# Self and cross attention as one stream of 120 steps, with the join and the query products between them as side work

## The reference

```python
h1 = _ln(x, n1_g, n1_b)
x = _attn(h1, h1, q1, k1, v1, o1_w, o1_b, heads) + x        # self: 512 keys
h2 = _ln(x, n2_g, n2_b)
x = _attn(h2, context, q2, k2, v2, o2_w, o2_b, heads) + x   # cross: 1024 keys
h3 = _ln(x, n3_g, n3_b)
...
ff = a * jax.nn.gelu(g, approximate=False) @ ff_w2 + ff_b2
return ff + x
```

## Time and profile before

| | us |
|---|---|
| median of 3 runs | 935.91 (933.89 to 936.53) |
| the profiled execution | 930.57 (span 928.8) |
| TensorE busy, share of the span | 844.5, 91% |
| VectorE busy | 617.0, 66% |
| ScalarE busy | 470.6, 51% |
| self steps (first exponential to the last values) | 375.5 to 489.8 |
| join and query products | 492.4 to 531.9 |
| cross prologue | 534.9 to 564.2 |
| cross steps | 564.2 to 783.3 |

### The profile page before, as it was taken

The page is one execution under the profiler, slowest core; times in us unless marked ns, Lnnn a source line. Parts: engine busy times, 40 slices in busy tenths (PEclk is TensorE's granted clock), DMA queues, the critical chain, the costliest instruction groups (busy, mean ns, idle before and its releaser), DMA issues.

```text
span 928.8 us, 11352 instructions
## 1 busy us (share of the span) xinstructions
PE 844.5 (91%) x4148; PEld 462.4 (50%) x4148; DVE 617.0 (66%) x1158; ACT 470.6 (51%) x682; POOL 78.2 (8%) x107
## 2 busy tenths in 40 slices
PE   4769989999999999999988699999999998699998
PEld 3646744444466675333324443333333333378988
DVE  4245547777583646799956597999999971656132
ACT  4523445454543441567785304766677777555030
POOL 3200000400004021000000300000000000120000
PEclk9979989999998997799999756999999999889999
DMA  6938768542401074222134320222222001400000
GB/s 222 271 102 239 230 169 254 174 116 60 118 26 41 21 231 124 65 70 70 37 66 73 109 72 1 53 53 53 53 53 53 2 2 43 198 1 1 29 1 29
DMA packets 30967, 83.18 MB, mean 90 GB/s; under 512 B 5173, under 2 KB 9213, under 8 KB 28607
## 3 DMA queue, kind: packets, MB, share of 16 engines
q1 hardware_dynamic: 30110, 79.71, 30.3%
q0 software_dynamic: 800, 2.73, 1.1%
HBM read 56.12 MB, written 25.89 MB: 88 GB/s over the span
## 4 chain that ended last, share of the span: by engine, by line
PE 60%; DVE 25%; DMA 6%; ACT 4%; issue 3%; POOL 1%; SPq 0%; DVEq 0%; ACTq 0%; POOLq 0%
PE PS L859 17%; PE PS L802 13%; DVE maxp L961 10%; PE PS L1376 8%; PE PS L553 8%; PE PS L839 6%; DVE negm L961 5%; PE PS L1388 4%; DMA k_d<-split 2%; PE PS L1200 2%; DMA ca_nat<-in_ca 2%; DVE turned L994 1%; ACT probs L925 1%; DVE out_t L1005 1%; DMA q_sl<-msplit 1%
## 5 line engine op out<-in xcount | busy, mean ns | idle before, releaser
L925 ACT ACTIVATE probs<-PS 128x1024 f32<-128x1024 f32 (+1 forms) x336 | 311.7, 971 | 150.0 <-PE PS L839 144.6
L961 DVE TENSOR_REDUCE maxp<-PS 128x1 f32<-128x512 f32 x448 | 280.1, 679 | 47.0 <-PE PS L802 46.0
L802 PE MATMUL PS<-k_sl,q_sl 48*128 48x512 f32 (+3 forms) x640 | 262.1, 489 | 24.4 <-DMA q_sl<-q_d 11.8
L802 PEld LDWEIGHTS PS<-k_sl,q_sl 48*128 48x128 f32 (+2 forms) x640 | 119.2, 199 | 201.5 <-DVE maxp L961 121.5
L839 PE MATMUL PS<-q_sl,k_sl 50*128 50x512 f32 (+3 forms) x672 | 203.2, 433 | 8.2 <-ACT probs L925 5.2
L961 DVE TENSOR_REDUCE negm<-PS 128x1 f32<-128x512 f32 (+1 forms) x192 | 121.0, 679 | 27.7 <-PE PS L802 27.6
L839 PEld LDWEIGHTS PS<-q_sl,k_sl 50*128 50x128 f32 (+2 forms) x672 | 102.6, 191 | 55.8 <-ACT probs L925 24.4
L859 PE MATMUL PS<-probs,v2c 128*32 128x512 f32 x640 | 87.4, 615 | 1.0
L591 DVE TENSOR_TENSOR split<-PS,split 128x512 fp32r<-128x512 f32 (+3 forms) x54 | 34.6, 649 | 47.9 <-ACT split L568 47.9
L859 PE MATMUL PS<-probs,v0c 128*64 128x512 f32 (+1 forms) x256 | 62.6, 610 | 0.0
L568 ACT CAST split<-PS 128x512 fp32r<-128x512 f32 (+3 forms) x54 | 29.8, 553 | 60.2 <-PE PS L553 51.7
(11 more groups left out here) (178 smaller groups left out, 981.0 us busy)
## 6 DMA issues: line engine op xcount, KB each, us to landing
k_d<-split SPq DMA_DIRECT2D x20, 512.0 KB, 3.6
q_d<-split SPq DMA_DIRECT2D x12, 512.0 KB, 3.1
k_sl<-k_d SPq DMA_DIRECT2D x8, 640.0 KB
k_sl<-k_d SPq DMA_DIRECT2D x40, 128.0 KB
q_sl<-q_d SPq DMA_DIRECT2D x40, 128.0 KB
k_sl<-k_d SPq DMA_DIRECT2D x20, 256.0 KB
w_raw<-in_ff_w SPq DMA_DIRECT2D x1, 3840.0 KB, 11.6
k_d<-split SPq DMA_DIRECT2D x10, 256.0 KB, 3.9
```

The lines of the kernel that those rows point to most:

```text
L802: nc.tensor.matmul(PS[0:a.qt, SBANKS[k % 3], 0:cn], q_view(g)[f:f + a.rows, j // a.stack, q * a.qt:(q + 1) * a.qt], k_view(g)[f:f + a.rows ...
L925: nc.scalar.activation(probs[0:a.size[t], x % PRING, :, 0:a.nq], PS[0:a.size[t], 2 * (x % 2):2 * (x % 2) + 2, 0:a.nq], ACT.Exp, scale=a.sc ...
L961: nc.vector.tensor_reduce((maxp if nch > 1 else negm)[0:a.qt, g.turn, o:o + 1], PS[0:a.qt, SBANKS[k % 3], 0:a.chunks[c][1]], AX.X, ALU.max ...
```

## The change

`S_SELF` and `S_CROSS` become one stream `S_REST` of 40 + 80 steps. The lead goes from 8 to 12 at step 39: four chunks (47 to 50) are issued there in a row, a "burst", after the values of step 39 and before the scores of step 40; chunks 40 to 46, also of cross attention, lie in steps 32 to 38. The first join's work and the query products are side tasks behind the maxima of named steps, in the maxima's three banks (`S1` = 20, `X0` = 40):

TensorE, the new order of a step:

```diff
             for s in range(len(st.steps)):
+                burst = st.burst_at(s)
+                if burst:
+                    for p in range(2):
+                        values(*st.steps[s], p)
+                for c in burst:
+                    maxima([c])
+                    flips([c])
+                    beside(st.burst_side.get(c, []))
...
                 maxima(st.chunks_at(s), 3)
                 flips(st.chunks_at(s))
+                beside(st.side.get(s, []))
```

A bank used by a side task is free when VectorE has added the product, when ScalarE has copied the turn, or when VectorE has subtracted a query's high part:

```diff
-                pe.wait_ge(st.score_free if by == "item" else st.flipped, n)
...
+                if by == "product":
+                    pe.wait_ge(join1.added, join1.base + n)
+                if by == "turn":
+                    pe.wait_ge(join1.ready, join1.base + n)
+                if by == "query":
+                    pe.wait_ge(crossp.low, n)
```

More of the change, by code:

```diff
@@ L863, in values, with beside @@
             mm.then_inc(st.used, 1)
+        def beside(tasks):
+            for kind, n in tasks:
+                k = st.side_use[kind, n]
+                bank = SBANKS[k % 3]
+                if kind == "product":
+                    pe_side_product(pe, n, bank, lambda: bank_free(k))
+                if kind == "turn":
+                    pe_side_turn(pe, n, bank, lambda: bank_free(k))
+                if kind == "query":
+                    pe_side_query(pe, n, bank, lambda: bank_free(k))
         for x in range(st.lead):
@@ L895, in pe_attention @@
                 maxima(st.chunks_at(s), 2, 3)
-                for p in range(2):
-                    values(*st.steps[s], p)
+                if not burst:
+                    for p in range(2):
+                        values(*st.steps[s], p)
                 maxima(st.chunks_at(s), 3)
                 flips(st.chunks_at(s))
+                beside(st.side.get(s, []))
     def act_attention(act, st, side=None):
@@ L963, in reduce, with maxima @@
                                     AX.X, ALU.max, negate=nch == 1).then_inc(st.score_free, 1)
-        def maxima(chunks, normalising=None):
-            if normalising is not None and normalising[1] == 0:
-                normalise(*normalising)
-                normalising = None
+        def maxima(chunks, first=(), second=(), third=()):
+            for part in first:
+                part()
+            todo = {1: list(second), 2: list(third)}
             for c in chunks:
@@ L1180, in build, with pe_side_product @@
     join2 = Join(3, w_out2, 2, 2, False)
+    side_stat, side_aggr = sem("side_stat"), sem("side_aggr")
+    side_root, side_inv = sem("side_root"), sem("side_inv")
+    def pe_side_product(pe, t, bank, bank_free):
+        b, c = t // 4, (t % 4) * 128
+        if t == 0:
+            pe.wait_ge(loaded_o1, 16)
+        if t % 4 == 0:
+            pe.wait_ge(A_SELF.out_done, join1.groups * (b + 1))
+        bank_free()
+        for g in range(join1.groups):
+            mm = nc.tensor.matmul(PS[:, bank, 0:D], out_t[:, b * join1.groups + g, c:c + 128], w_out1[:, g, :],
+                                  start=(g == 0), stop=(g == join1.groups - 1))
+        mm.then_inc(join1.product, 1)
```

287 lines of the change are left out of this document (206 added, 81 removed).

## The result

The changed kernel took 940.0 us (median of 17 runs, 935.5 to 944.3), the kernel before 936.3 (17 runs beside it): ratio 1.0043, 95% interval 1.0024 to 1.0061. A gain of 16 us was forecast and a loss of 4 measured, above the range of 906 to 934. The profiled execution of after has a span of 938.7 us and a time of 940.54.

The account below looks back on a forecast made before the run. Plain steps of 2.70 us were taken as balanced, TensorE working 2.45, VectorE 2.4; VectorE bound the prologue. 64.4 - 24.3 - 1 - 22.1 - 1 = 16.0 us gained: 914.6 profiled, 920.0 at the median, range 906 to 934.

Parts of the forecast that it names:

- the clock, a term of 1 us: Around the burst: a stretch at the low clock level costs 1 us, nothing at the least, 4 at most.
- The walk through the steps: Side work followed step by step through engines and bank waits: 24.3 us in batch 0, 22.1 in batch 1.
- Part 1: Self step 32 to cross step 43: merged stages take 44.0 us in place of 108.4, gaining 64.4 before side work.
- Part 3, batch 0: Self steps 21 to 29: products, turns and query products as side work cost 24.3 us.
- The store wait: Step 29: query 2's copy waits for query 0's store, queued behind group 8's loads, costing 3.3 us beyond the product.
- Part 4: Burst and cross steps to 49: batch 1's side work and the last self group's transposes cost 22.1 us.
- Rival (c): Clock stays low through steps 21 to 48, costing 24 us: 8 slower, 944 at the median; chance 0.08.
- Rival (b): Every wait between engines 0.5 us longer over some 25 side tasks, or group 10's load late: 12 us more, 932; chance 0.17.
- The rule weighed: ScalarE table switches cost 1.28 us plus a 1.38 drain each: up to 5.5 us more, about 925.5; a row spoke against it.
- Rival (d): Each ScalarE table switch drains, two of four or all on the path: 923 to 925.5; chance 0.04.
- Rival (a): Side work overlaps better, banks free sooner, costing only 29.3 us: gain 35, 900.6 at the median; chance 0.18.
- Rival (e): Cross maxima don't start before the join, and the burst grows to a prologue: about 20 us stay, 940; chance 0.05.

Follow-up runs that it names:

- kernel with the store first: The changed kernel with SyncE issuing the stores of queries 0 and 1 ahead of the loads of group 8's maxima: 0.9994 of the kernel before.
- the best version: The changed kernel with query stores first, side tasks spread, products and queries mid-step, statistics behind each add, two extra matmuls per burst maximum: 929.8 us, 0.9915 of before.

## Why the prediction was wrong, step by step

The miss is 20.0 us at the medians. By kernels that leave work out it is 3.9 in the merged stages (57.2 for 61.1) and 16.1 in the side work (61.2 for 45.1). By the table of stages it is 5.5 (a wrong row) + 6.9 (batch 0) + 1.9 (burst) + 7.8 (cross steps) - 0.3. The two sums differ by 1.8, less than what the unchanged stages of two profiled executions differ by: from the end of step 56 on and ahead of step 21, after took 5.1 us more than before, of which about 1.0 is the weight split. The profiled execution of before, at 930.57, is faster than all of its 17 later runs (931.25 to 942.59), so differences are taken from the medians and stages, not from that time.

Two steps of the prediction failed: a row read as the wrong step, 5.5 us, and above all the clock, a term of 1 us that measures about 14.5 (an estimate, worked out below). The walk through the steps was right to 1 or 2 us wherever the clock was up.

- **Part 1, the stages that fall together: right in sum, wrong in its left end.** Steps 32 to 39 took 20.3 (forecast 20.6) and the merged kernel gained 57.2. The failing step is "Between self step 32 (465.62) ... and cross step 43 (574.01) ... lie 108.4 us": the row is that of step 30. Counting steps from a row whose number is sure, and once more from the other side, would have shown it.
- **Part 3, batch 0: 24.3 forecast, 31.2 measured, and most of the excess is the clock.** Steps 21 to 29, counted by TensorE's first scores, took 56.1 and not 50.7: steps 21 to 23, at the high level, 17.7 for a forecast of 18.6, but 24 to 27 took 26.1 for 19.6. The forecast had the clock at 1.00 there; it fell. Three executions have the same work in self steps 21 to 32 (but for the root's table, missing in the second) and differ in the clock, the first number behind the busy times: after, the kernel without that table, and that with the extra matmuls (which lie behind this stretch).

```profile
442.10:506.10 64.00, 54.16 (x242) 24.18 (x242) 40.79 (x83) 32.91 (x48) 5.92 (x7) 0.87 0.23 61
```

```profile
442.70:509.50 66.80, 56.92 (x242) 26.11 (x242) 40.79 (x83) 30.49 (x46) 6.18 (x7) 0.82 0.21 58
```

```profile
445.00:513.60 68.60, 60.12 (x242) 27.20 (x242) 40.80 (x83) 32.88 (x47) 5.91 (x7) 0.78 0.20 54
```

  Low time is 17.1, 23.9 and 30.7 us, so each us of it costs about 0.35. Taken back to none, after's 64.0 become some 58 against the 57.1 forecast: about 6 of the 6.9 us are the clock, an estimate from single executions. What is left, about 1, is all that the walk's hand-overs can have been short of. Steps 24 to 26, with two turns a step, are where they may be: they took 17.9 in after for a forecast of 13.0, with 10.0 of low time. The store wait was foreseen; its price of 3.3 can't be checked to better than the 4.6 above.
- **Part 4, burst and batch 1: 1.9 and 7.8 over, nearly all of it the clock.** The walk (nine plain steps at 25.5, and +11.2) gave 36.7 for steps 41 to 49; they took 41.9. The burst took 25.3 for 23.4. With the two extra matmuls in the burst, the same cross steps 40 to 56 ran with no low time. The windows of after, and of that kernel:

```profile
551.70:619.20 67.50, 60.64 (x295) 25.10 (x294) 48.31 (x90) 41.73 (x57) 11.45 (x13) 0.86 0.18 41
```

```profile
557.00:618.10 61.10, 53.60 (x295) 22.32 (x294) 48.19 (x90) 41.71 (x56) 11.44 (x13) 1.00 0.20 45
```

  The same work took 61.1 and not 67.5, for 18.3 us of low time less: 0.35 us for each again. Burst and cross steps together took 84.2 there, against 82.1 forecast without the term for the clock, and 92.8 in after.
- **The clock, the term of 1 us.** This is the worst sized of the terms. In the burst a single product takes 3.25 us, where a pair takes 3.50 in step 21 at the high level, and VectorE waits 3.27 for the next maximum:

```profile
536.41 3.25 PE L1284 MATMUL PS<-w_out,out_t 128*128 128x320 f32 x6 [0.23 <-DVE maxp L1024]
...
540.13 0.69 DVE L1024 TENSOR_REDUCE maxp<-PS 128x1 f32<-128x512 f32 x1 [3.27 <-PE PS L842]
```

  The low level then stays through steps 40 to 42 (0.52 from 552 to 567). The kernel with the store first has the same code there, and its clock is 0.95 behind the burst. Exponentials of steps 40 and 41, in after and then in that kernel:

```profile
551.67 1.94 ACT L986 ACTIVATE probs<-PS 128x1024 f32<-128x1024 f32 x2 [15.19 <-PE PS L879]
558.29 1.94 ACT L986 ACTIVATE probs<-PS 128x1024 f32<-128x1024 f32 x2 [4.68 <-PE PS L879]
```

```profile
553.44 1.94 ACT L986 ACTIVATE probs<-PS 128x1024 f32<-128x1024 f32 x2 [15.19 <-PE PS L879]
557.96 1.94 ACT L986 ACTIVATE probs<-PS 128x1024 f32<-128x1024 f32 x2 [2.58 <-PE PS L879]
```

  6.62 against 4.52; over steps 40 to 46 it is 31.3 against 26.7. In sum: about 6 in batch 0, 2.2 in the burst (25.3 for 23.1 with the extra matmuls, which had 9.0 us of low time less there) and 6.4 behind it, 14.5 where 1 was forecast and 4 allowed. After has 51 us of low time between steps 21 and 56, in pieces. Before had 48, of them 39 ahead of step 40 in its prologue, where VectorE was the bound and the low level cost nothing that shows. The low time was not made, it was moved to where TensorE is the bound. The medians agree in kind: over after's 17 runs, which spread over 9 us, the span grows by about 0.3 us for each us of low time.
- **Rival (c)** had this mechanism, at 0.08. It wanted the low level through steps 21 to 48; that it came in pieces makes its 24 us some 14.5, and the row of part 1 gives the rest of the loss. **Rival (b)**, every hand-over longer than in the walk, at 0.17 and 12 us, is not what happened: about 1 us is left for it in batch 0 and up to 2 in batch 1.
- **The rule weighed.** The Trainium skill (ScalarE: Activation LUTs, What ACT_TABLE_LOAD costs) adds a drain of 1.38 us to each load. No row here shows it (the root begins 0.01 us behind its load), and leaving all four loads out changed neither step clock. Rival (d) falls.
- **Rival (a)**, better overlap, falls: the side work cost 61 and not 29. **Rival (e)** falls: the cross maxima do start in step 32, and the burst has 16 of them.
- **The range.** The gain of 16 was the difference of two large terms. The first, 64.4, was 5.5 too high, 9% of it; the second, 45.1 for the side work of both batches, came out at 61.2, 36% more. The 14 us above the forecast allowed for 31% on the second alone, and for nothing on the first.

What stays open: why the clock falls in batch 0. From 471.0 to 484.6 it was low in after, and nearly every kernel with turns in batch 0 has a low stretch about there; the one with products alone has none. So no execution of this code has steps 24 to 26 at the high level throughout, and their split into clock and hand-overs rests on the price of 0.35. And whether the extra matmuls help at all at the medians: the best version lies 2.3 us under the same kernel without them, and the intervals overlap.

## What to carry to other kernels

Work put into a pipeline whose engines hand over through three banks in strict order does not hide in their idle time, since each task passes through the engines one after the other: a walk that adds up the hand-overs gave 45 us, where the same work as a block took 39.5 (45.1 with its gaps), and at the high level of the clock the walk held to 1 or 2 us. The runs paid 61, because TensorE was at the low level for part of the side work. So price such a move in two parts: the hand-overs, and then the clock, with about 0.3 to 0.35 us for each us of low time in steps that TensorE bounds. A stretch in which TensorE only feeds VectorE drops to the low level for free (0.51 in the old prologue); output products placed in it take nearly twice as long (3.25 us for one, 3.50 for two at the high level), so they belong where the clock is up. Test the two halves apart (the stages merged with no side work, then the side work added kind by kind), since the gain is a small difference of two large numbers, and compare stage times only together with the low time of each execution.

## What the runs showed of the hardware

- **The low level costs this stream about 0.35 us per us**: batch 0 took 64.0, 66.8 and 68.6 us at a granted clock of 0.87, 0.82 and 0.78, the cross steps 61.1 and 67.5 at 1.00 and 0.86, with the same work. **A plain self step at the low level takes 4.2 us, not 2.7**, where rival (c) had taken 3.56. ScalarE in the kernel with the store first, start of the self stage:

```profile
388.86 1.94 ACT L986 ACTIVATE probs<-PS 128x1024 f32<-128x1024 f32 x2 [2.32 <-PE PS L879]
393.02 1.94 ACT L986 ACTIVATE probs<-PS 128x1024 f32<-128x1024 f32 x2 [2.22 <-PE PS L879]
397.18 1.94 ACT L986 ACTIVATE probs<-PS 128x1024 f32<-128x1024 f32 x2 [2.22 <-PE PS L879]
```

- **A VectorE instruction took three times as long beside a GpSimd one that shares no data with it.** The normalised rows take 0.44 us, but once 1.40, ending 0.19 behind a GpSimd subtraction of the query input's low part; the change moved that subtraction to GpSimd. Nine more of these kernels show such a row, of 1.23 to 1.40 us, always beside that subtraction; the kernel before shows none. In after:

```profile
472.43 0.44 DVE L1353 TENSOR_SCALAR xhat<-resid,mv,rstd 128x320 f32<-128x320 f32 x1
...
473.01 1.40 DVE L1353 TENSOR_SCALAR xhat<-resid,mv,rstd 128x320 f32<-128x320 f32 x1
```

```profile
472.93 1.29 POOL L1400 TENSOR_TENSOR act_low<-act_t,x_high 128x512 fp32r<-128x512 f32 x1 [0.47 <-ACT x_mixed L1388]
```

  The Trainium skill (SBUF — State Buffer, SBUF: two separate sides) describes the pair of ports that the two engines share as a lock held for a whole instruction; by that, the trace agrees. No experiment tried it.
